# Cross-attention with image tokens: bias through the output product, context loads on GpSimd, and a new order of transfers, rounds and first steps

## What is computed

```python
q = split_heads(x @ w_q)
k, v = split_heads(text @ w_k), split_heads(text @ w_v)
out_text = softmax(q @ k.T / 4) @ v
k_ip, v_ip = split_heads(ip_h @ w_k_ip), split_heads(ip_h @ w_v_ip)
out_ip = softmax(q @ k_ip.T / 4 + mask_ip) @ v_ip
out = (merge(out_text) + merge(out_ip)) @ w_out + b_out + x
```

## Time and profile before

| What | Value |
| --- | --- |
| median of three runs | 1266.85 us |
| the profiled execution | span 1263.2 us from first to last instruction, 34240 instructions; the median of the runs, 3.65 us more, stands for its whole time, which the profile does not give |
| busy: PE, DVE, POOL, ACT | 1158.1, 1044.3, 904.7, 897.6 us |
| first block | 0 to 46 us |
| the rounds | 46 to 225.4 us |
| steps -2 and -1, and the wait before step 0 | 225.4 to 260.6 us |
| steps 0 to 65 | 260.6 to 1263.2 us |

### The profile page before, as it was taken

How to read it: one execution, slowest core, us unless ns; L and a number is a source line. 1 busy time by engine, 2 the same in 40 slices (tenths; PEclk the granted TensorE clock), 3 DMA queues, 4 the chain that set the end, 5 groups by cost and what they waited for, 6 DMA issues and landing times.

```text
span 1263.2 us, 34240 instructions
## 1 busy us (share of the span) xinstructions
PE 1158.1 (92%) x12734; PEld 1114.9 (88%) x12734; DVE 1044.3 (83%) x2054; ACT 897.6 (71%) x1923; POOL 904.7 (72%) x1004
## 2 busy tenths in 40 slices
PE   6998887559999999999999999999999999999996
PEld 5898787459999999999999999999999999999985
DVE  5687975669888889888898888888888888898972
ACT  2343343448888888877888888888888888887773
POOL 0111101038889889988988988898898899898896
PEclk9999999779999999999999999999999999999998
DMA  6388887645555545544455554454555555555431
GB/s 173 66 181 168 156 182 149 102 91 111 116 116 120 120 114 121 120 115 114 114 120 120 121 117 115 115 116 115 117 117 115 118 120 117 123 117 114 102 82 61
DMA packets 361460, 151.31 MB, mean 120 GB/s; under 512 B 298640, under 2 KB 350864, under 8 KB 360016
## 3 DMA queue, kind: packets, MB, share of 16 engines
q1 hardware_dynamic: 361296, 149.13, 52.9%
HBM read 88.17 MB, written 39.90 MB: 101 GB/s over the span
## 4 chain that ended last, share of the span: by engine, by line
PE 53%; POOL 11%; DMA 11%; SPq 9%; DVE 6%; issue 5%; ACT 2%; POOLq 0%; ACTq 0%; DVEq 0%
PE ps_a L832 9%; DMA q_hi_extra<-q_hi_lo 8%; PE ps_o L903 8%; PE ps_s L873 7%; PE ps_m L854 6%; PE ps_s L879 6%; PE ps_b L832 6%; POOL prob_lo L1402 6%; PE ps_k L199 2%; PE ps_v L199 2%; SPq L617 2%; SPq L668 2%; POOL y L1396 2%; DMA x_keep<-in_x_dram 2%; PE ps_a L918 2%
## 5 line engine op out<-in xcount | busy, mean ns | idle before, releaser
L1402 POOL TENSOR_TENSOR prob_lo<-prob,prob_hi 128x512 f16<-128x512 f32 (+1 forms) x448 | 506.1, 1148 | 106.0 <-ACT prob_hi L1071 106.0
L873 PE MATMUL ps_s<-q_hi_lo,keys 128*128 128x256 f32 x960 | 248.9, 299 | 44.3 <-DMA q_hi_extra<-q_hi_lo 42.9
L1070 ACT ACTIVATE prob<-ps_s 128x512 f32<-128x512 f32 (+1 forms) x448 | 254.2, 567 | 35.4 <-PE ps_s L879 31.0
L1071 ACT ACTIVATE prob_hi<-ps_s 128x512 f16<-128x512 f32 (+1 forms) x448 | 252.8, 564 | 0.0
L879 PE MATMUL ps_s<-q_hi_extra,keys 128*128 128x256 f32 x960 | 234.1, 281 | 0.3 <-ACT q_hi_extra L1058 0.3
L1298 DVE TENSOR_REDUCE stats<-ps_m 128x8 f32<-128x552 f32 x320 | 231.2, 722 | 0.0
L873 PEld LDWEIGHTS ps_s<-q_hi_lo,keys 128*128 128x128 f32 x960 | 172.6, 190 | 54.1 <-issue 37.4
L903 PE MATMUL ps_o<-values,prob_hi 128*128 128x68 f16 (+7 forms) x3584 | 200.9, 193 | 1.5 <-DVE heads L1312 1.5
L903 PE MATMUL ps_o<-values,prob_lo 128*128 128x68 f16 (+3 forms) x1792 | 190.8, 193 | 0.0
L903 PEld LDWEIGHTS ps_o<-values,prob_hi 128*128 128x128 f16 x3584 | 174.9, 98 | 13.0 <-issue 1.6
L879 PEld LDWEIGHTS ps_s<-q_hi_extra,keys 128*128 128x128 f32 x960 | 173.5, 190 | 0.5 <-ACT q_hi_extra L1058 0.5
(11 more groups left out here) (180 smaller groups left out, 2999.1 us busy)
## 6 DMA issues: line engine op xcount, KB each, us to landing
x_in<-in_x_dram SPq DMA_DIRECT2D x64, 320.0 KB, 3.8
q_hi_extra<-q_hi_lo SPq DMA_DIRECT2D x64, 320.0 KB, 3.4
x_keep<-in_x_dram SPq DMA_DIRECT2D x64, 320.0 KB, 3.2
out_dram<-y SPq DMA_DIRECT2D x128, 160.0 KB, 1.8
k_scratch<-k_stage SPq DMA_DIRECT2D x16, 770.0 KB, 5.8
keys<-k_scratch SPq DMA_DIRECT2D x256, 48.1 KB, 2.1
ctx_in<-in_ctx_dram SPq DMA_DIRECT2D x64, 128.0 KB, 2.8
keys<-k_scratch SPq DMA_DIRECT2D x256, 24.1 KB, 1.9
```

What stands on the lines that cost most here:

```text
L873: mm(ps, keys[:, n, 0, quad, c:c + P], q_hl[n][:, quad, :], start=i == 0, stop=False)
L1070: nc.scalar.activation(prob[:, s, 0:w], ps_s[(b[1] + s) % 2][:, 0:w], ACT.Exp)
L1071: nc.scalar.activation(prob_hi[par(b)][:, s, 0:w], ps_s[(b[1] + s) % 2][:, 0:w], ACT.Exp).then_inc(s_hi, 1)
L1402: nc.gpsimd.tensor_tensor(prob_lo[par(b)][:, s, 0:w], prob[:, s, 0:w], prob_hi[par(b)][:, s, 0:w], ALU.subtract).then_inc(s_lo, 1)
```

## The change

- **Bias.** `b_out` is split in high and low part and written into rows 0 and 32 of `wo_lo`'s third part, beside zeros; the third part of the attention is kept as two tiles, and rows 0 and 32 of the second are ones. `add_bias` on POOL goes. The third part of the split changes places (the product count stays 8).
- **Transfers.** `x_in` has 320 columns instead of 384 (a second copy of the last 64 is no longer loaded, nor for `w_q`). In a step SP issues `copy_q(b+1)`, then the store of b-3, the residual of b-1, the keys of b+2, the values of b+2, `x` of b+4. Tails of the second half are stored one a step from step 1 to 7.
- **Context.** POOL issues `load_pair` for pairs 4 to 31.
- **Rounds.** PE transposes both next pairs before both value products; ACT and DVE follow that order, and DVE sums the context after both `v_lo`.
- **First steps.** In the last round PE transposes `x` of batch 0 before the value products, and makes its queries; steps -2 and -1 become one written-out `first`. The second half's `tail_hi` are in `first`, `tail_lo` at the end of DVE's steps 0 and 1.
- **Smaller ones.** `stats` has 64 columns instead of 128; `spread_values` covers only slots in use (50 of 65) in five instructions.

```diff
@@ layout @@
-R_MT, R_MI, R_MASK, R_ONE = 64, 64 + H, 64 + 2 * H, 64 + 2 * H + NIP
+R_MT, R_MI, R_MASK, R_ONE = 0, H, 2 * H, 2 * H + NIP
+NSTAT = 64
+SPREADS = [[(0, 3, 5, 3), (12, 1, 1, 2)], [(1, 3, 5, 5)], [(2, 3, 1, 4), (7, 3, 1, 4)]]
...
@@ SP, rounds and after @@
                     for i in range(NI):
-                        for u in range(2):
-                            if 2 * i + u + 4 < 2 * NI:
-                                sp.wait_ge(s_t, 2 * i + u + 1)
-                                sp.wait_ge(s_sum, 2 * i + u + 1)
-                                load_pair(sp, 2 * i + u + 4)
                         load_main(i)
...
                             store_tail(*early_tail(i))
+                    copy_q((None, 0, 1))
+                    sp.wait_ge(s_xt, 1)
+                    load_x((None, 2, 1))
                     load_keys((None, 1, 1))
+                    sp.wait_ge(s_xt, 2)
+                    load_x((None, 3, 1))
                     load_values((None, 1, 1))
 
                     def step(sp, b, n):
-                        E, A, Bs, Cs, Ds = has(n)
-                        if A:
+                        if n < 0:
+                            return
+                        if n + 1 < NB:
                             copy_q(off(b, 1))
-                        if n is None or n + 4 < NB:
+                        if 0 <= n - 3 < NB:
+                            store(off(b, -3), 0)
+                            store(off(b, -3), 1)
+                        if 0 <= n - 1 < NB:
+                            load_residual(off(b, -1))
+                        if 3 <= n + 2 < NB:
+                            sp.wait_ge(s_sc, at(b, PAIRS, 0))
+                            load_keys(off(b, 2))
+                        if 2 <= n + 2 < NB:
+                            sp.wait_ge(s_vx, at(b, 3, 3))
+                            load_values(off(b, 2))
+                        if n + 4 < NB:
                             sp.wait_ge(s_xt, at(b, 1, 3))
                             load_x(off(b, 4))
-                        if Ds:
-                            store(off(b, -2), 0)
-                            store(off(b, -2), 1)
-                        if Bs:
-                            load_residual(b)
-                        if n is None or 0 <= n < NB - 2:
-                            sp.wait_ge(s_vx, at(b, 3, 3))
-                            load_values(off(b, 2))
-                        if n is None or 0 <= n < NB - 3:
-                            sp.wait_ge(s_sc, at(b, PAIRS, PAIRS))
-                            load_keys(off(b, 3))
-                        if n in (0, 1):
-                            for u in range(4 * n, min(4 * n + 4, len(TILES_IN))):
-                                store_tail(1, u)
+                        if 0 <= n - 1 < len(TILES_IN):
+                            store_tail(1, n - 1)
...
@@ PE @@
-                        for u in range(2):
-                            if i + 1 < NI:
+                        if i + 1 < NI:
+                            for u in range(2):
                                 transposes(2 * (i + 1) + u)
-                            project_values(i, u)
+                            for u in range(2):
+                                project_values(i, u)
...
-                            last = nc.tensor.transpose(ps_b[:, c:c + P], x_in[par(b)][:, t, 256:DW], ident[:])
+                            last = nc.tensor.transpose(ps_b[0:DL, c:c + P], x_in[par(b)][:, t, 256:D], ident[:])
...
-                        terms += [(both, w[n][:, 2, cols]) for n in range(2)]
+                        terms += [(third_hi, w[0][:, 2, cols]), (third_lo, w[1][:, 2, cols])]
...
+                    def first(e, a):
+
+                        x_transpose(a, -2)
+                        for u in range(2):
+                            project_values(NI - 1, u)
+                        for m in range(3):
+                            project(a, m)
+                        x_transpose(e, -1)
+                        max_scores(a, 0)
+                        max_scores(a, 1)
+                        project(e, 0)
+                        max_scores(a, 2)
+                        max_scores(a, 3)
+                        project(e, 1)
+                        max_scores(a, 4)
+                        project(e, 2)
+                        stats_transpose(a)
...
@@ DVE @@
+                    def split_out(raw):
+
+                        then(nc.vector.tensor_copy(wo[0][:, 0:2, :], raw[:, 0:2, :]))
+                        nc.vector.tensor_tensor(wo[1][:, 0:2, :], raw[:, 0:2, :], wo[0][:, 0:2, :].bitcast(fp32), ALU.subtract)
+                        nc.vector.tensor_copy(wo[0][0:64, 2, :], raw[0:64, 2, :])
+                        then(nc.vector.tensor_copy(wo[1][64:P, 2, :], raw[64:P, 2, :]))
+                        then(nc.vector.tensor_tensor(wo[0][64:P, 2, :], raw[64:P, 2, :], wo[1][64:P, 2, :].bitcast(fp32), ALU.subtract))
+                        nc.vector.memset(wo[1][0:64, 2, :].bitcast(fp32), 0.0)
+                        then(nc.vector.tensor_copy(bias_hl[0].bitcast(f32r), bias[:]))
+                        then(nc.vector.tensor_tensor(bias_hl[1], bias[:], bias_hl[0], ALU.subtract))
+                        nc.vector.tensor_copy(wo[1][0:1, 2, :], bias_hl[0][0:1, :])
+                        then(nc.vector.tensor_copy(wo[1][32:33, 2, :], bias_hl[1][32:33, :]))
...
-                        for u in range(2):
-                            if i + 1 < NI:
+                        if i + 1 < NI:
+                            for u in range(2):
                                 context_lo(2 * (i + 1) + u)
-                            v_lo(2 * i + u)
-                            if i + 1 < NI:
+                            for u in range(2):
+                                v_lo(2 * i + u)
+                            for u in range(2):
                                 sum_context(2 * (i + 1) + u)
                         prepare_main(i)
...
+                    def first(e, a):
+
+                        x_lo(a)
+                        for u in range(2):
+                            v_lo(2 * (NI - 1) + u)
+                        for m in range(3):
+                            q_lo(a, m)
+                        maxima(a, 0)
+                        x_lo(e)
+                        maxima(a, 1)
+                        maxima(a, 2)
+                        q_lo(e, 0)
+                        maxima(a, 3)
+                        maxima(a, 4)
+                        image_maxima(a)
+                        q_lo(e, 1)
+                        q_lo(e, 2)
...
+                        def bias_rows():
+                            for q in range(4):
+                                dve.wait_ge(s_vst[q], 32 * (2 * NI // 4))
+                            nc.vector.memset(aT2[1][0:64, :].bitcast(fp32), 0.0).then_inc(s_z, 1)
+                            dve.wait_ge(s_z, 3)
+                            for r in (0, 32):
+                                nc.vector.memset(aT2[1][r:r + 1, :].bitcast(fp32), 1.0).then_inc(s_z, 1)
...
+                            for t, count, stride, slots in SPREADS[g]:
+                                tt = slice(t, t + (count - 1) * stride + 1, stride)
+                                last = nc.vector.tensor_tensor(
+                                    v[:, tt, 0:slots, 2:SLOT],
+                                    raw_v[par(b)][:].rearrange("p t (o c) -> p t o c", o=1)[:, tt].broadcast_to([P, count, slots, 2 * DH]),
+                                    own[:, tt, 0:slots, :], ALU.mult)
...
@@ POOL @@
                     for i in range(NI):
+                        for u in range(2):
+                            if 2 * i + u + 4 < 2 * NI:
+                                pool.wait_ge(s_t, 2 * i + u + 1)
+                                pool.wait_ge(s_sum, 2 * i + u + 1)
+                                load_pair(pool, 2 * i + u + 4)
                         if i >= 2:
                             pool.wait_ge(s_kst[i % 2], 16 * (i // 2))
...
-                        def add_bias():
-                            pool.wait_ge(s_xk[par(c)], nth(c, 16))
-                            nc.gpsimd.tensor_tensor(x_keep[par(c)][:], x_keep[par(c)][:],
-                                                    bias[:].rearrange("p (o d) -> p o d", o=1).broadcast_to([P, NT, D]),
-                                                    ALU.add).then_inc(s_xb, 1)
```

More of the change, by code:

```diff
@@ L88 @@
 VCOLS = TILES * SLOTS * SLOT
+SPREADS = [[(0, 3, 5, 3), (12, 1, 1, 2)], [(1, 3, 5, 5)], [(2, 3, 1, 4), (7, 3, 1, 4)]]
+assert all(NSLOTS[t + n * d] == slots for group in SPREADS for t, count, d, slots in group for n in range(count))
 def bank_tiles(half):
@@ L860, in stats_transpose @@
                         for t in range(NT):
[L861 removed]
+                            last = nc.tensor.transpose(ps_m[0:NSTAT, 0, t * P:(t + 1) * P], stats[:, t, :], ident[:])
                         last.then_inc(s_et, 1)
```

(10 more changed lines are left out.)

263 lines of the change are left out of this document (143 added, 120 removed).

## The result

| What | before | after |
| --- | --- | --- |
| median, run side by side | 1269.78 us | 1287.10 us |
| range of the runs | 1266.1 to 1284.12 | 1283.86 to 1287.91 |
| span of the profiled execution | 1263.2 us | 1286.0 us |
| step 0's first score product | 260.59 us | 243.96 us |
| from there to the transpose of the statistics of batch 3 | 42.77 us | 55.30 us |

The ratio of after to before is 1.0149, with a 95% interval of 1.0129 to 1.0169. The last four rows add up: -16.6 + 12.5 + 26.2 + 0.7 = 22.8 us, the difference of the spans. The way to step 0 became shorter, by 16.6 us of the 24.8 that were forecast for rounds and start together; the first steps lost most of that again; and each of 60 periods became longer where it was to become 0.58 us shorter.

What follows compares the result with a forecast made beforehand. PE was taken as the bound, with a floor of 14.70 us a step. Span 1263.2 - 35 (steps) - 7.5 (rounds) - 17.3 (start) - 2.5 (end) = 1200.9, plus 3.65 around it: 1204.6, say 1205 us; range 1186 to 1228.

Steps and rivals of the forecast that it cites:

- so it saves about 0.35 and DVE has 13.25: DVE's spreading in the steps: 50 of 65 slots in five instructions saves about 0.35 us a step, leaving DVE 13.25.
- another engine takes the steps: First rival: another engine than PE sets the steps at 15.1 us each, time 1225 us; chance 0.17.
- The loop of SP's queue: Steps: POOL's end, 15 issues, query copy, scores, exponentials; opened by the new order, period 15.36 to 14.78 us, gain 35.
- The second loop: Steps: POOL's end, store, residual's load, bias addition (1.56 us after 0.74 of waiting), rest of POOL's step.
- SP's wait for POOL's addition shrinks to under 60 us.: Sign that the forecast is right: SP's wait at the output stores, 304.7 us before, falls under 60 us.
- lie in steps 0 and 1, where DVE has no norm or low attention to do: First steps: DVE's deferred tails, 13 x 0.54 = 7 us, fall where DVE lacks its norm and low attention work.
- The rounds: Before step 0: context loads on POOL and the new order of PE gain 7.5 us, bounds 0 and 18.
- second and fourth rival: Second: context late from POOL, 1227 us, chance 0.08. Fourth: POOL's dear issues bound the rounds, 1304 us, 0.03.
- Step 0: Start of the steps: 18 us after PE's last value product instead of 35, gain 17 (bounds 13 and 21).
- The end: Last steps: without POOL's bias additions in steps 63 and 64, gain 2.5 us (bounds 1 and 4).

Runs made afterwards that it cites:

- e1: The changed kernel with the spreading of values as before (three instructions, all 5 slots): 1220.0 us, ratio to before 0.9641.
- e9: e1 with SP's order of before in a step: 1265.07 us, ratio to before 0.9987, period 15.38 us.
- e10: e1 with a 128x640 addition on POOL where the bias addition stood: 1233.32 us, ratio to before 0.9741, period 14.81 us.
- e11: e1 with both SP's old order in a step and the addition on POOL: 1267.55 us, ratio to before 1.0016, period 15.39 us.
- e5: e1 with all low tails of the second half at the end of DVE's `first`, before step 0: 1206.55 us, ratio to before 0.9488.
- e2: The kernel before with only the five-instruction spreading over the slots in use put in: 1354.98 us, ratio 1.0703.
- e14: e6 with the context loads of the rounds back on SP: 1212.78 us, ratio to before 0.9576.
- e8: The changed kernel with one spreading instruction of 2080 elements at the head of DVE's step: 1254.95 us (one run), period 15.22 us.
- e6: e5 with `v_lo` and the context sums pair by pair in the rounds, as before: 1203.05 us, ratio to before 0.9456.
- e12: e6 with SP issuing batch 0's query copy and some first loads ahead of the last value stores, batch 1's values and copy between the last two: 1202.80 us.
- e13: e12 with DVE's tails one unit at a time between the maxima of steps 0 and 1: 1204.03 us.

## Why the prediction was wrong, by its own steps

- **"so it saves about 0.35 and DVE has 13.25"** (the spreading). This step failed, and it decided the sign. It scaled 2.38 us by 50/65 and gave each of two more instructions 0 to 0.2 us. Measured: 4.21 us where 2.03 were forecast, +1.8 us a step instead of -0.35, and 15.2 us of DVE in a period of 15.8. The row it rested on the earlier trace rows was itself part waiting (0.8 of 2.38 us), which grows with the number of instructions. Its bounds held no collision, though the earlier trace rows mixes two forms: split by form, before has 969 ns for 800 elements and 449 for 480, 2.2 times the time for 1.7 times the size. Cost: 60 x (15.80 - 14.68) = 67 us, all of e1's gain over after.
- **"another engine takes the steps"**, the first rival, was right in kind. Its price, 15.1 us a step, was far too low, because it too took DVE's load as given.
- **The loop of SP's queue.** Right: a floor of 14.70 forecast, 14.68 measured (e1); no PE wait for the query copy after step 0; the period without the new spreading 0.10 under the 14.78 taken, and back at 15.38 with the old order alone (e9). The second loop, through POOL's bias addition, was right too: it closes at 14.81 (e10) and lay hidden behind the first (e11).
- **"SP's wait for POOL's addition shrinks to under 60 us."** Wrong in size: 170.1 us from 304.7. It cost nothing, as what stands behind it is early enough; a sign that was no sign.
- **The deferred tails "lie in steps 0 and 1, where DVE has no norm or low attention to do".** Failed: 13.4 us (e5). DVE had the idle time, but the tails stood at the step's end in one block, ahead of the next step's first maxima. They took 10.1 us for 13, 0.78 each, where the earlier trace rows has 0.54.
- **The rounds.** Forecast 7.5 us of gain. PE's last value product starts at 221.67 for 225.22, 3.5 us; but the nine other profiles with the same rounds have 218.6 to 221.1, and e2, with the rounds of before, 227.8. Between the means, 220.0 and 226.5, it is 6.5 us, so the forecast holds within that scatter. Context waits gone (e14: 11.6 us, forecast 11.3). `batch_sums` waits 12.0 us in 14 pieces, 0.86 a round, forecast 0.75; 8.3 us of waits for `ctxT_lo` stay, forecast 5. POOL's issues cost 0.57 us each, not 1. The loads land after 4.3 us (median, 2.8 from SP's queue before), yet PE waits for none of them, and SP waits once, 5.3 us, for POOL's copy of the key tails. The second and fourth rival fall.
- **Step 0** at 243.96, forecast 230 to 240. It starts 22.3 us after the last value product for 35.4 before, a gain of 13.1 and so at the bound of the forecast's 17. The copy is issued behind the last stores, as forecast, but these end 17.7 us after that product, not 13. The keys behind it cost 1.95 us, forecast 1.7. The granted clock was 0.79 from 222 to 244 us, for 0.68 in the last stretch of the earlier trace rows; what that gave back, forecast 2 us, was not separated.
- **The end**: forecast 2.5 us of gain, measured none (38.7 for 38.0). With the addition back it is 2.5 us longer in e10 than in e1 and 4.8 longer in e11 than in e9, but the kernels without it differ among themselves by 4.0 (35.8 in e14, 39.9 in e8). Left open.

With the two failed terms out of the kernel (e5: three instructions, tails early) the time is 1206.55 us, for a forecast of 1205. The miss of 82 us is 67 for the spreading, 13 for the tails, and 1 or 2 of the rest. That the rest comes so near is in part luck, as its errors cancel: by e5's profile the stretch up to batch 3's transpose gave 18.4 us of the 24.8 forecast for rounds and start, and the end 1.1 of 2.5, but the 60 periods gave 41.4 where 35 were forecast.

The POOL rows of after that bear on the two rivals:

```profile
L196 POOL DMA_DIRECT2D ctx_in<-in_ctx_dram x56 | 31.5, 571 | 141.4 <-DVE context_sums L1235 141.4
...
ctx_in<-in_ctx_dram POOLq DMA_DIRECT2D x56, 128.0 KB, 4.3
```

The best version that was run is e6, 1203.05 us, with e12 (1202.80), and by their intervals e5 and e13, not to be told from it: the change without its new spreading, without the deferral of the tails into the steps, and with the sums pair by pair.

## What to carry to other kernels

Do not scale a VectorE instruction by its elements while GpSimd works beside it: split its group by form, compare with a moment at which GpSimd is idle, and count instructions as well as elements when both inputs are in SBUF. Idle time of an engine with a fixed order is no room for work unless the work stands where the idle time is; look at what the block stands ahead of. And when one loop is opened, look for the next one close behind it: here the second stood 0.13 us above the floor. A table that saves a quarter of the elements for two more instructions was here worth minus 67 us beside a queue order worth 42.

## What the runs showed that was not expected

- A 64-element multiplication on DVE takes 858 ns on average beside GpSimd's work, of which its own part is about 0.1 us; two 384s take 1.47 us beside GpSimd's subtractions and 0.70 beside its memset.
- GpSimd's memset of 128x512 f16 takes 525 ns (its subtraction 1.17 us when nothing holds it up) and leaves DVE's two-input instructions at full speed.
- GpSimd waits for DVE as DVE waits for GpSimd: in e8 the addition of `y` that meets the 2080-element instruction takes 1.87 us instead of 0.87.
- Fewer microseconds on DVE can give a slower kernel: e8 has 13.1 us of DVE in a step and a period of 15.22, e1 13.6 us and 14.68.
